# Expert tiles of a small vision transformer: first layer, transpositions and second layer all in 64-row products

## The reference

```python
# D = 192, M = 768, G = 4, E = 8, KG = 2, KE = 4
ggates, gidx = _topk_gates(xf @ Wg + bg, KG)
egates, eidx = _topk_gates(jnp.einsum('nd,gde->nge', xf, We) + be, KE)
...
for g in range(G):
    h = jax.nn.gelu(jnp.einsum('nd,edm->enm', xf, W1[g]) + b1[g][:, None, :], approximate=False)
    o = jnp.einsum('enm,emd->end', h, W2[g]) + b2[g][:, None, :]
    y = y + jnp.einsum('end,ne->nd', o, combine[:, g, :])
```

## Time and profile before

| | us |
|---|---|
| median of 3 runs (lowest, highest) | 784.41 (782.96, 785.36) |
| span of the profiled execution, first to last instruction | 782.1 |
| PE busy / PE weight loads busy | 672.5 / 571.2 |
| DVE / ACT / POOL busy | 426.2 / 236.5 / 323.5 |
| expert loop, first weight load of L1484 to the last of L1492's | 399.7 to 772.2 |

### The profile page before, as it was taken

The page is one execution under the profiler, slowest core; times in us unless marked ns, Lnnn a source line. Parts: engine busy times, 40 slices in busy tenths (PEclk is TensorE's granted clock), DMA queues, the critical chain, the costliest instruction groups (busy, mean ns, idle before and its releaser), DMA issues.

```text
span 782.1 us, 19902 instructions
## 1 busy us (share of the span) xinstructions
PE 672.5 (86%) x6348; PEld 571.2 (73%) x6348; DVE 426.2 (55%) x1247; ACT 236.5 (30%) x673; POOL 323.5 (41%) x265
## 2 busy tenths in 40 slices
PE   5957858898989996863379899999999999999995
PEld 5724646656745885753269789999999999999994
DVE  7574583745479559977934344444444434434342
ACT  3112312123247211111433333333343333333331
POOL 4730730011023322520334456555564655655554
PEclk9976968577999998975579999999999999999998
DMA  9900000000000030013116765464545665565432
GB/s 349 255 2 3 3 3 2 3 1 3 1 1 1 1 122 1 1 68 132 30 31 164 217 170 116 119 182 81 164 113 161 172 169 161 115 163 114 103 50 38
DMA packets 34982, 70.05 MB, mean 90 GB/s; under 512 B 6353, under 2 KB 21234, under 8 KB 34930
## 3 DMA queue, kind: packets, MB, share of 16 engines
q0 software_dynamic: 15840, 17.71, 13.5%
q10 hardware_dynamic: 8064, 33.12, 12.6%
q1 hardware_dynamic: 11026, 18.48, 7.3%
HBM read 59.31 MB, written 9.98 MB: 89 GB/s over the span
## 4 chain that ended last, share of the span: by engine, by line
PE 62%; DVE 17%; DMA 6%; issue 4%; POOL 1%; ACTq 1%; ACT 1%; DVEq 0%; POOLq 0%
PE bank L1492 17%; PE bank L1484 12%; PE bank L1487 7%; PE bank L1340 4%; PE bank L1469 3%; PE bank L1272 3%; PE bank L1292 3%; DMA arena<-normed_rows,fetch_u 3%; PE bank L1356 2%; DMA out_dram<-arena,number_u 2%; PE bank L1310 1%; PE bank L1283 1%; DVE zx L894 1%; DVE arena L1097 1%; DVE arena L1094 1%
## 5 line engine op out<-in xcount | busy, mean ns | idle before, releaser
L631 POOL DMA_INDIRECT out_dram<-arena,number_u x80 | 127.0, 1587 | 51.6 <-DMA out_dram<-arena,number_u 26.3
L625 POOL DMA_INDIRECT arena<-normed_rows,fetch_u x80 | 78.3, 979 | 114.9 <-DMA out_dram<-arena,number_u 51.0
L1179 DVE COPY arena<-bank 128x256 f32<-128x256 f32 x81 | 34.4, 425 | 119.5 <-PE bank L1469 110.8
L796 ACT ACTIVATE arena<-bank,arena 128x128 f32<-128x128 f32 x234 | 64.5, 375 | 115.5 <-PE bank L1487 115.5
L1492 PE MATMUL bank<-arena 128*128 128x192 f32 x468 | 83.0, 326 | 0.1
L1492 PEld LDWEIGHTS bank<-arena 128*128 128x128 f32 x468 | 75.4, 190 | 0.5 <-ACT arena L796 0.5
L1197 DVE TENSOR_SCALAR arena<-bank,arena 128x192 f32 x80 | 33.4, 418 | 59.1 <-PE bank L1492 57.5
L533 POOL TENSOR_SCALAR rstd<-mv 128x4 f32<-128x4 f32 x12 | 2.7, 229 | 147.5 <-DVE mv L883 147.5
L1484 PE MATMUL bank<-arena 128*128 128x128 f32 x468 | 59.1, 276 | 1.4 <-DVE arena L1179 1.1
L1484 PEld LDWEIGHTS bank<-arena 128*128 128x128 f32 x468 | 56.9, 192 | 3.0 <-issue 1.5
L796 ACT ACTIVATE arena<-bank,w_space 128x128 f32<-128x128 f32 x132 | 36.5, 375 | 67.0 <-PE bank L1487 67.0
(11 more groups left out here) (241 smaller groups left out, 1263.8 us busy)
## 6 DMA issues: line engine op xcount, KB each, us to landing
arena<-in_moe_w_dram ACTq DMA_DIRECT2D x14, 579.0 KB, 6.1
arena<-in_moe_w_dram ACTq DMA_DIRECT2D x14, 576.0 KB, 4.2
arena<-in_xf_dram SPq DMA_DIRECT2D x8, 512.0 KB, 9.8
w_space<-in_moe_w_dram ACTq DMA_DIRECT2D x7, 579.0 KB, 5.8
w2small<-in_moe_w_dram ACTq DMA_DIRECT2D x7, 579.0 KB, 5.6
w_space<-in_moe_w_dram ACTq DMA_DIRECT2D x7, 576.0 KB, 4.2
wab<-in_moe_w_dram ACTq DMA_DIRECT2D x7, 576.0 KB, 4.3
arena<-in_w_dram SPq DMA_DIRECT2D x8, 480.0 KB, 9.1
```

The source lines that it names most:

```text
L625: pool.indirect_dma_start(out=mo_stage[:, s * ROWN:(s + 1) * ROWN], out_offset=None, in_=normed_rows, in_offset=bass.IndirectOffsetOnAxis( ...
L631: pool.indirect_dma_start(out=out, out_offset=bass.IndirectOffsetOnAxis(ap=number_u[:, s:s + 1], axis=0), in_=mo_res[:, s * D:(s + 1) * D] ...
L796: nc.scalar.activation(mo_hT[:, m, :], bank[2 + m][:, 0:P], ACT.Gelu, bias=b1[:, m:m + 1]).then_inc(free[2 + m], 1)
L1179: nc.vector.tensor_copy(mo_xT.rearrange("p k t -> p (k t)"), bank[1][:, 0:2 * P]).then_inc(free[1], 1)
```

## The change

The 192 features become three blocks of 64, all handled by the 64-row form.

- `mo_x` holds each block twice side by side, `mo_xT` holds for each block (index `k`) the 64 features on partitions 0 to 63 and again on 64 to 127. The weights of the first layer are laid out anew on the host: even chunks on partitions 0 to 63, odd chunks on 64 to 127 (the number of bytes is the same).
- The first layer is 18 products of 64 rows: chunk pair (4, 5) first, then (0, 1), then (2, 3); three blocks each, the two row halves in turn. Chunks 4 and 5 go to banks 3 and 7; 0 and 2 share bank 2, 1 and 3 share bank 6, and these two banks are declared full only when all four chunks are.
- The transposition is six of 64 rows x 128 columns, into banks 1 and 4 (tokens 0 to 63, and 64 to 127).
- The second layer splits each chunk's 128 hidden features in halves, summed in bank 0 and in bank 5, chunk order 4, 5, 0, 1, 2, 3. VectorE adds the two banks with one more instruction.
- Gelus run in the same new order.

```diff
-W1N = HID + MC // 2 * P
+HF = P // 2
+XB = D // HF
+W1N = D // 64 * (MC // 2) * P
+HID_BANK = {0: (2, 0), 2: (2, P), 4: (3, 0), 1: (6, 0), 3: (6, P), 5: (7, 0)}
+HID_ORDER = (4, 5, 0, 1, 2, 3)
+HID_READ = {4: (1, 1), 5: (1, 1), 0: (2, 1), 1: (2, 1), 2: (2, 2), 3: (2, 2)}
+COL_BANK, SUM_BANK = (1, 4), (0, 5)
...
-                    act.wait_ge(full[0], i + moe_base[0])
-                    for m in range(MC):
-                        act.wait_ge(full[2 + m], i + (moe_base[2 + m] + 1))
-                        nc.scalar.activation(mo_hT[:, m, :], bank[2 + m][:, 0:P], ACT.Gelu, bias=b1[:, m:m + 1]).then_inc(free[2 + m], 1)
+                    for b in SUM_BANK:
+                        act.wait_ge(full[b], i + moe_base[b])
+                    for m in HID_ORDER:
+                        b, c = HID_BANK[m]
+                        act.wait_ge(full[b], i + (moe_base[b] + 1))
+                        nc.scalar.activation(mo_hT[:, m, :], bank[b][:, c:c + P], ACT.Gelu, bias=b1[:, m:m + 1]).then_inc(free[b], 1)
...
-                nc.vector.tensor_copy(mo_x[:, D:2 * P], mo_stage[:, bass.ds(i % STAGE * ROWN + P, REST)])
-                nc.vector.tensor_copy(mo_x[:, 0:D], mo_stage[:, bass.ds(i % STAGE * ROWN, D)]).then_inc(sem("rows_staged"), 1)
+                nc.vector.tensor_copy(mo_x.rearrange("p (k o x) -> p k o x", k=XB, o=2),
+                                      repeat(mo_stage[:, bass.ds(i % STAGE * ROWN, D)].rearrange("p (k x) -> p k x", k=XB), 2, 2)).then_inc(sem("rows_staged"), 1)
...
-                dve.wait_ge(full[1], i + (moe_base[1] + 1))
-                nc.vector.tensor_copy(mo_xT.rearrange("p k t -> p (k t)"), bank[1][:, 0:2 * P]).then_inc(free[1], 1)
+                for b in COL_BANK:
+                    dve.wait_ge(full[b], i + (moe_base[b] + 1))
+                for g, b in enumerate(COL_BANK):
+                    nc.vector.tensor_copy(mo_xT[:, :, g * HF:(g + 1) * HF], bank[b][:, 0:D].rearrange("p (k t) -> p k t", k=XB)).then_inc(free[b], 1)
...
+                    dve.wait_ge(full[SUM_BANK[1]], upper)
+                    dve.wait_ge(free[SUM_BANK[0]], lower)
+                    stt(out=mo_new[:, bass.ds(new, D)], in0=bank[SUM_BANK[1]][:, 0:D], scalar=mo_gates[:, bass.ds(gate, 1)], in1=mo_new[:, bass.ds(new, D)],
+                        op0=ALU.mult, op1=ALU.add).then_inc(free[SUM_BANK[1]], 1)
...
-                for k in range(2):
-                    ins = nc.tensor.transpose(bank[1][:, k * P:(k + 1) * P], mo_x[:, k * P:(k + 1) * P], ident[:])
-                ins.then_inc(full[1], 1)
+                pe.sem_inc(sem("turning"), 1)
+                for k in range(XB):
+                    for g, b in enumerate(COL_BANK):
+                        r = g * HF
+                        ins = nc.tensor.transpose(bank[b][:, k * HF:(k + 1) * HF], mo_x[r:r + HF, k * P:(k + 1) * P], ident[r:r + HF, r:r + HF])
+                        if k == XB - 1:
+                            ins.then_inc(full[b], 1)
...
-                    for m in range(MC):
-                        mm(bank[2 + m][:, 0:P], w1e[:, m * P:(m + 1) * P], mo_xT[:, 0, :], start=True, stop=False)
-                    for m in range(MC):
-                        r, c = m % 2 * REST, HID + m // 2 * P
-                        mm(bank[2 + m][:, 0:P], w1e[r:r + REST, c:c + P], mo_xT[r:r + REST, 1, :], start=False, stop=True).then_inc(full[2 + m], 1)
+                    for j in (2, 0, 1):
+                        for k in range(XB):
+                            for g in range(2):
+                                r, (b, c) = g * HF, HID_BANK[2 * j + g]
+                                ins = mm(bank[b][:, c:c + P], w1e[r:r + HF, j, k, :], mo_xT[r:r + HF, k, :], start=(k == 0 and c == 0), stop=(k == XB - 1), skip_group_check=(j < 2))
+                                if k == XB - 1 and j:
+                                    ins.then_inc(full[b], 1)
                     transpose_rows(i + 1)
-                    pe.wait_ge(free[0], i + moe_base[0])
-                    for m in range(MC):
-                        pe.wait_ge(free[2 + m], i + (moe_base[2 + m] + 1))
-                        ins = mm(bank[0][:, 0:D], mo_hT[:, m, :], w2e[:, m, :], start=(m == 0), stop=(m == MC - 1))
-                    ins.then_inc(full[0], 1)
+                    for b in SUM_BANK:
+                        pe.wait_ge(free[b], i + moe_base[b])
+                    for n, m in enumerate(HID_ORDER):
+                        hb, (per, nth) = HID_BANK[m][0], HID_READ[m]
+                        pe.wait_ge(free[hb], i * per + (moe_base[hb] + nth))
+                        for g, b in enumerate(SUM_BANK):
+                            r = g * HF
+                            ins = mm(bank[b][:, 0:D], mo_hT[r:r + HF, m, :], w2e[r:r + HF, m, :], start=(n == 0), stop=(n == MC - 1))
+                            if n == MC - 1:
+                                ins.then_inc(full[b], 1)
```

More of the change, by code:

```diff
@@ L271, in vit_tower @@
         mo_gates = view(P, 4 * NE)
-        mo_x = view(P, 2 * P)
-        mo_xT = view(P, 2 * P).rearrange("p (k t) -> p k t", k=2)
+        mo_x = view(P, 2 * D)
+        mo_xT = view(P, XB * P).rearrange("p (k t) -> p k t", k=XB)
         mo_res = view(P, 2 * D)
@@ L786, in expert @@
                 if e and e + AHEAD - 1 < NE:
-                    act.wait_ge(full[0], first + moe_base[0])
+                    for b in SUM_BANK:
+                        act.wait_ge(full[b], first + moe_base[b])
                     load_expert(act, (u + AHEAD - 1) % AHEAD, e + AHEAD - 1)
@@ L1171, in stage_rows @@
                 dve.wait_ge(sem("rows_in"), i * 16 + 16)
-                dve.wait_ge(full[1], i + moe_base[1])
+                for b in COL_BANK:
+                    dve.wait_ge(full[b], i + moe_base[b])
                 nc.vector.tensor_copy(mo_gates[:, bass.ds(i % 4 * NE, NE)], mo_stage[:, bass.ds(i % STAGE * ROWN + D, NE)])
-                nc.vector.tensor_copy(mo_x[:, D:2 * P], mo_stage[:, bass.ds(i % STAGE * ROWN + P, REST)])
-                nc.vector.tensor_copy(mo_x[:, 0:D], mo_stage[:, bass.ds(i % STAGE * ROWN, D)]).then_inc(sem("rows_staged"), 1)
+                nc.vector.tensor_copy(mo_x.rearrange("p (k o x) -> p k o x", k=XB, o=2),
+                                      repeat(mo_stage[:, bass.ds(i % STAGE * ROWN, D)].rearrange("p (k x) -> p k x", k=XB), 2, 2)).then_inc(sem("rows_staged"), 1)
             def take_columns(i):
-                dve.wait_ge(full[1], i + (moe_base[1] + 1))
-                nc.vector.tensor_copy(mo_xT.rearrange("p k t -> p (k t)"), bank[1][:, 0:2 * P]).then_inc(free[1], 1)
+                for b in COL_BANK:
+                    dve.wait_ge(full[b], i + (moe_base[b] + 1))
+                for g, b in enumerate(COL_BANK):
+                    nc.vector.tensor_copy(mo_xT[:, :, g * HF:(g + 1) * HF], bank[b][:, 0:D].rearrange("p (k t) -> p k t", k=XB)).then_inc(free[b], 1)
             dve.wait_ge(sem("table_ready"), 1)
@@ L1192, in _ @@
                     new = dve.snap(i % 4 * D)
-                    added, summing = dve.snap(i + 1), dve.snap(i + (moe_base[0] + 1))
+                    added = dve.snap(i + 1)
+                    lower, upper = [dve.snap(i + (moe_base[b] + 1)) for b in SUM_BANK]
                     half, tile, ahead = dve.snap(i % 2), dve.snap(i + 0), dve.snap(i + 4)
                     nc.vector.tensor_copy(fetch_u[:, bass.ds(half, 1)], table_u[:, bass.ds(ahead, 1)]).then_inc(sem("fetch_set"), 1)
-                    dve.wait_ge(full[0], summing)
-                    ts(out=mo_new[:, bass.ds(new, D)], in0=bank[0][:, 0:D], scalar1=mo_gates[:, bass.ds(gate, 1)], scalar2=None, op0=ALU.mult).then_inc(free[0], 1)
+                    dve.wait_ge(full[SUM_BANK[0]], lower)
+                    ts(out=mo_new[:, bass.ds(new, D)], in0=bank[SUM_BANK[0]][:, 0:D], scalar1=mo_gates[:, bass.ds(gate, 1)], scalar2=None, op0=ALU.mult).then_inc(free[SUM_BANK[0]], 1)
+                    dve.wait_ge(full[SUM_BANK[1]], upper)
+                    dve.wait_ge(free[SUM_BANK[0]], lower)
+                    stt(out=mo_new[:, bass.ds(new, D)], in0=bank[SUM_BANK[1]][:, 0:D], scalar=mo_gates[:, bass.ds(gate, 1)], in1=mo_new[:, bass.ds(new, D)],
+                        op0=ALU.mult, op1=ALU.add).then_inc(free[SUM_BANK[1]], 1)
                     dve.sem_inc(sem("scaling"), 1)
@@ L1467, in transpose_rows @@
                 pe.wait_ge(sem("rows_staged"), i + 1)
-                for k in range(2):
-                    ins = nc.tensor.transpose(bank[1][:, k * P:(k + 1) * P], mo_x[:, k * P:(k + 1) * P], ident[:])
-                ins.then_inc(full[1], 1)
+                pe.sem_inc(sem("turning"), 1)
[5 more added lines that the diff above has]
+                            ins.then_inc(full[b], 1)
             tile_starts += [expert_start(pe, e, 1) for e in range(18, 25)]
-            pe.wait_ge(free[1], moe_base[1])
+            for b in COL_BANK:
+                pe.wait_ge(free[b], moe_base[b])
             transpose_rows(0)
```

(18 more changed lines are left out.)

6 lines of the change are left out of this document (2 added, 4 removed).

## The result

The changed kernel takes 803.6 us (median of 4 runs, 799.8 to 806.9) against 784.9 us: ratio 1.024, 95% interval 1.020 to 1.028. It is 2.4% slower; the forecast was 763 us, and the range (754 to 779) does not hold it. The profiled execution has a span of 798.0 us.

A forecast was written before the change was run, and what follows sets the result against it. TensorE was taken to bound the expert loop, 80 tiles of 4.53 us. Terms: -27.3 (shorter tile) + 1.6 (sequencer) + 0.5 (VectorE) + 4 (PoolE, DMA) = -21 from the 784.4 us median, giving 763 us; 8-in-10 range 754 to 779.

The forecast's parts named there:

- TensorE's tile, 4.19 us: Expert loop: first layer 2.06, transpositions 0.23, second layer 1.90 us; 4.19 instead of 4.53, saving 27.3 us over 80 tiles.
- holes: Two 0.20 us losses per tile at 128/64-row changes, forecast to vanish; rival that they stay: 791 us, chance 0.06.
- don't overlap: Rival: second-layer pairs of 192 columns do not run beside each other, up to +1.95 us a tile; 913 us, chance 0.06.
- Inside 4.19. Hidden: VectorE's chain per tile grows from 2.8 to about 3.6 to 4.0 us, hidden except +0.5 us once after the last tile.
- ScalarE, costed at nothing: Gelu 0 ends at 2.74 us, wanted by the second layer at 2.88; 0.14 us slack, tight, no cost.
- The sequencer, +1.6: TensorE's sequencer at late experts' starts, already late, falls 0.2 us further behind, 8 times: +1.6 us.
- PoolE and the DMA, +4: Some 6 to 12 tiles run at the DMA's period while weights arrive and do not shrink: 4 us of gain lost.
- the forecast's own terms without PoolE's: TensorE's shorter tile -27.3, its sequencer +1.6, VectorE behind the last tile +0.5 us; PoolE and DMA's +4 left out.
- fed late: Rival: slow transpositions, late Gelu 0, sequencer or PoolE make the tile 4.30 to 4.40 us; say 773 us, chance 0.32.
- slower: Outcome slower than before, chance 0.10, from holes staying and second-layer pairs not overlapping, with some of "fed late".

The follow-up runs named there:

- e4: Changed kernel with the transpositions back as three full 128-row products into one bank and one copy of the columns: 800.5 us, ratio 1.018.
- e11: Kernel before the change with plain transfers in place of PoolE's indirect gather and accumulate (timing only): 775.5 us, ratio 0.990.
- e10: Changed kernel with plain transfers in place of PoolE's indirect gather and accumulate (timing only): 766.8 us, ratio 0.980.
- e9: Changed kernel without the TensorE sequencer's own post (turning), the wait for the rows moved to a first-layer product; chip 0: 777.8 us, ratio 0.993.
- p3: e9's kernel, unaltered, run on chip 12: 805.4 us, ratio 1.030.
- p2: The changed kernel, unaltered, run on chip 12: 804.3 us, ratio 1.024.
- p1: The kernel before the change, unaltered, run on chip 12: 786.8 us, ratio 1.003.
- p4: e9's kernel with VectorE's tile loop rotated (columns of tile i+2 taken at the end of tile i), on chip 12: 801.3 us, ratio 1.025.
- g1: Changed kernel with PoolE's accumulate as a plain transfer, the gather still indirect (timing only), on chip 15: 773.3 us, ratio 0.989.
- g2: Changed kernel with both PoolE transfers plain (timing only) and VectorE's loop rotated, columns taken at the body's end; chip 15: 777.3 us, ratio 0.992.
- e1: Changed kernel with the second layer back in 128-row products into one bank, without the second sum: 830.9 us, ratio 1.058.

## Why the forecast was wrong, step by step

- **TensorE's tile, 4.19 us: right.** 4.19 without a gap ahead, in all kernels with this TensorE loop; no holes; transpositions at 0.11, 0.06, 0.06; second-layer pairs at 0.1625. The rule of the Trainium skill ("TensorE: Matmul & The Clock Gate", "LDWEIGHTS (loading the stationary operand)") has 107 ns for each such load; as an estimate, 0.32 us for the three pairs. The trace does not agree: from the first transposition's load (459.21) to the second layer's (459.44) it is 0.23 us. The rival "don't overlap" (913) is out. The holes come with the change of row split (e4 has them).
- **"Inside 4.19. Hidden" (VectorE): the step that failed in the kernel.** Copies and sums were about right: columns done 3.31 us after the tile's start (3.3 forecast), an unhindered chain of 3.4 us (3.6 to 4.0). What was left out is the register work at a change of expert: leaving the inner loop and loading two values, 2.1 us, 32 times. The trace of the kernel before has the loads:

```profile
L1187 DVEq TENSOR_LOAD <-starts x32: 298/306/499, 401.9 to 761.4; - x32
```

  The kernel before hid the work. In an ordinary tile its columns lay ready 1.2 us before they were wanted; at a change VectorE started on them 3.46 us after the tile's first load (e11), and they were wanted at 4.53. In the changed kernel, where the second sum and the second copy make VectorE's tile longer, it starts at 4.17, is done at 4.79, and they are wanted at 4.19 (e10). That costs (4.84 - 4.19) x 25 = 16 us by e10's trace; in the seven late experts it is hidden. This is read from the trace and not shown by removing it, as the one edit that tried moved it. The sum bears it out: with plain transfers, where no post is late, e11's 775.5 and the forecast's own terms without PoolE's give 775.5 - 27.3 + 1.6 + 0.5 + 16 = 766.3, and e10 took 766.8.
- **ScalarE, costed at nothing: right** where posts come on time. There TensorE's loads waited for it twice in 350 us, 1.5 us (e9, chip 0); the same kernel on chip 12, with late posts, has 22 such waits and 11.3 us (p3). The 13.7 us of the changed kernel's profile are of that kind.
- **The sequencer, +1.6: about right.** TensorE's first layer waited 2.9 us for it before (8 times) and 4.1 us in e10 (7 times): 1.2 us more.
- **PoolE and the DMA, +4: about right.** Plain transfers gain the changed kernel 11 us (777.8 to 766.8, chip 0; e9 and e10 differ in the post too, which p2 and p3 show to be idle) and the kernel before 8. So the real transfers take about 3 us of the change's gain (1.5 with e9's 776.2).
- **A term that was not there: held posts.** This is what took the time out of the range. e9's kernel takes 777.8 us on chip 0, inside it, and 805.4 on chip 12: 28 us. The kernel before takes 783.4 beside e9 and 784.3 beside p1 to p4 (786.8 in p1's own runs): it has the same mechanism (53 late posts in p1), but fewer of its posts are held (25 of 70 inside an accumulate, for 114 of 127 in p2; why fewer is open), and it has 1.2 us of slack behind the columns where the changed one has 0.8. A late post costs what exceeds the slack; how much of the 28 us each of the two differences makes is not shown. The trace of before that the forecast had shows no late post.

Sum: 763 + 16 = 779 without held posts; e9 gave 777.8. With them it is 804 to 805 on chip 12 (p2, p3), and 803.6 was measured. Of my rivals "fed late" had the direction (columns late), at a quarter of the size; "slower" had the wrong mechanism.

What stays open: how and by what an indirect transfer of PoolE holds TensorE's posts, and whether it is the chip or the state in which it stood, as each chip was seen once. The changed kernel itself, with the sequencer's post, was not run on chip 0. No version with PoolE's real transfers beat the kernel before on a chip that holds posts (e9 did on chip 0, by 0.7%); what might (the two table values loaded where VectorE idles, columns taken two tiles ahead with a second buffer) was not tried.

## What to carry to other kernels

Shortening the bounding engine's loop by 0.34 us takes 0.34 us from every slack around it (the columns': 1.2 to 0.8): list what each other engine does at the rare turns of a loop too (leaving it, loading values), not only in a plain tile. If a wait grows that names no releaser, compare the time of the post with the end of its matmul, and look at what other engines do in between. And an edit that seems to mend a kernel on one chip is tested against the unmended one on the same chip before it is believed.

## What the runs showed of the hardware that I had not expected

- While PoolE works on an indirect transfer, the semaphore posts of TensorE's products may be held until about its end (in p2 83 of the 114 in an accumulate came within 0.2 us of its end; in g1 those in a gather came mostly 0.3 to 0.5 us behind its end): on chips 6, 9 and 12, in the changed kernel and its versions, 77 to 91% of the posts that ended in an accumulate's first 1.35 us came late, up to 2.3 us where a gather and an accumulate follow each other; on chip 15 84% of those in a gather's later part did (g1). On chip 0 none of 149 did (e9). Plain transfers that PoolE issues, through the same kind of queue, hold none (g2: 0 of 117 that ended in one).
- TensorE itself goes on meanwhile: loads and products stay 0.11 us a pair; only the news of them is late, and comes in order, 34 to 43 ns apart.
- Such delays seem to lock in: in e1 late columns put PoolE's next transfers into the same place of the next tile, and 57 of 79 tiles took over 5.2 us. That one causes the other is my reading of the trace.
- Leaving an inner loop and entering it again with two loaded bounds keeps VectorE from its next copy for 2.1 us (e10), 0.3 us of it for each of the two loads.
